# The first two turns of a fused attention and ternary-FFN kernel written out in an order of their own, with two weight quarters loaded to other places and Sign in place of Relu and clip

## The reference, cut to what matters

```python
# x: (8, 1024, 512); 8 heads of 64; segments of 128 tokens, walked in order with a memory per head
q, k, v = xs @ Wq, xs @ Wk, xs @ Wv
att_mem = (elu(q)+1) @ mem / ((elu(q)+1) @ z)          # mem, z: of the segments before
mem += (elu(k)+1).T @ v ;  z += (elu(k)+1).sum()
att = sigmoid(betas) * att_mem + (1 - sigmoid(betas)) * (softmax(q @ k.T / 8) @ v)
x = layernorm(x + att.reshape(...) @ Wo)
Wq1, Wq2 = clip(round(W / (mean(|W|) + 1e-5)), -1, 1)   # W1: 2048x512, W2: 512x2048
out = layernorm(x + relu(x @ Wq1.T + b1) @ Wq2.T + b2)
```

## Time and profile before

| | us |
|---|---|
| median of 3 runs (1894.05 to 1895.91) | 1894.54 |
| the profiled execution's own time | 1894.47 |
| its span, first to last instruction | 1892.5 |
| PE busy in the span | 1848.2 (98%) |
| DVE busy | 1450.5 (77%) |
| ACT busy | 1001.9 (53%) |
| POOL busy | 765.2 (40%) |

### The profile page before, as it was taken

The page is one execution under the profiler, slowest core; times in us unless marked ns, Lnnn a source line. Parts: engine busy times, 40 slices in busy tenths (PEclk is TensorE's granted clock), DMA queues, the critical chain, the costliest instruction groups (busy, mean ns, idle before and its releaser), DMA issues.

```text
span 1892.5 us, 44351 instructions
## 1 busy us (share of the span) xinstructions
PE 1848.2 (98%) x16447; PEld 1306.4 (69%) x16447; DVE 1450.5 (77%) x2935; ACT 1001.9 (53%) x2422; POOL 765.2 (40%) x775
## 2 busy tenths in 40 slices
PE   5789999999999999999999999999999999999998
PEld 3666677776667776667776677776677776677765
DVE  7868777778777778777777777778777778777774
ACT  5765555555555555555555555555555555555541
POOL 1214334444334444334444334444334444344442
PEclk9899999999999999999999999999999999999999
DMA  8422333422333323323322333323333323233110
GB/s 272 125 44 33 62 58 62 68 48 52 63 59 60 68 44 55 64 55 64 68 47 51 64 59 60 68 48 52 60 62 60 68 47 52 59 59 63 36 24 23
DMA packets 556420, 117.47 MB, mean 62 GB/s; under 512 B 529824, under 2 KB 533808, under 8 KB 555696
## 3 DMA queue, kind: packets, MB, share of 16 engines
q1 hardware_dynamic: 556208, 114.64, 30.9%
HBM read 50.54 MB, written 16.80 MB: 36 GB/s over the span
## 4 chain that ended last, share of the span: by engine, by line
PE 93%; DVE 4%; ACT 1%; SPq 1%; issue 1%; DMA 0%; another core or an unknown queue 0%; POOLq 0%; DVEq 0%; POOL 0%; ACTq 0%
PE bank L433 12%; PE bank L434 12%; PE bank L449 11%; PE bank L450 11%; PE bank L282 6%; PE bank L283 6%; PE bank L284 6%; PE bank L370 3%; PE bank L415 3%; PE bank L414 3%; PE bank L413 3%; PE bank L296 3%; PE bank L349 3%; PE bank L298 3%; PE bank L297 3%; PE bank L401 2%
## 5 line engine op out<-in xcount | busy, mean ns | idle before, releaser
L433 PE MATMUL bank<-yt,w1t 128*128 128x256 f16 x2048 | 453.9, 273 | 0.3 <-DVE yt L811 0.2
L434 PE MATMUL bank<-yt,w1t 128*128 128x256 f16 x2048 | 453.9, 273 | 0.0
L1154 ACT ACTIVATE prob<-bank,exp_bias,gscalars 128x128 f32<-128x128 f32 x512 | 227.7, 456 | 360.4 <-DVE exp_bias L728 356.2
L449 PE MATMUL bank<-w2t,arena 128*128 128x512 f16 x1024 | 388.4, 379 | 0.0
L450 PE MATMUL bank<-w2t,arena 128*128 128x512 f16 x1024 | 388.1, 379 | 0.0
L1198 ACT ACTIVATE arena<-bank,b_scaled,wscalars 128x256 f32<-128x256 f32 x512 | 263.0, 570 | 205.3 <-PE bank L434 151.8
L863 DVE CAST arena<-arena 128x512 f16<-128x512 f32 x256 | 154.3, 603 | 92.8 <-ACT arena L1198 92.0
L1323 POOL TENSOR_TENSOR att_mem<-att_mem,gate_in 128x512 f32<-128x512 f32 x60 | 86.6, 1444 | 330.5 <-DVE att_mem L767 320.2
L433 PEld LDWEIGHTS bank<-yt,w1t 128*128 128x128 f16 x2048 | 200.5, 98 | 23.8 <-issue 0.6
L434 PEld LDWEIGHTS bank<-yt,w1t 128*128 128x128 f16 x2048 | 200.3, 98 | 22.7
L1401 POOL TENSOR_TENSOR arena<-arena 128x512 f16<-128x512 f32 x128 | 155.2, 1213 | 86.1 <-DVE arena L863 86.1
(11 more groups left out here) (186 smaller groups left out, 4299.9 us busy)
## 6 DMA issues: line engine op xcount, KB each, us to landing
rows<-in_L_attn_x SPq DMA_DIRECT2D x32, 512.0 KB, 3.8
out_rows<-rows SPq DMA_DIRECT2D x64, 256.0 KB, 2.3
x_blocks<-in_L_attn_x SPq DMA_DIRECT2D x248, 64.0 KB, 3.0
sk<-sk_t SPq DMA_DIRECT2D x480, 32.0 KB, 2.0
att_dot<-att_mem SPq DMA_DIRECT2D x480, 32.0 KB, 2.0
y_blocks<-rows SPq DMA_DIRECT2D x480, 32.0 KB
arena<-in_L_ffn_W SPq DMA_DIRECT2D x6, 1024.0 KB, 5.3
w2t<-in_L_ffn_W SPq DMA_DIRECT2D x2, 1024.0 KB, 13.1
```

Source lines behind the costliest of these rows:

```text
L433: pe.matmul(ps[:, c], w1t[:, k, cols], yt[:, g % 2, :, k], start=k == 0, stop=False)
L434: ins = pe.matmul(ps[:, c], w1t[:, k, cols], yt[:, g % 2, :, KT + k], start=False, stop=k == KT - 1)
L449: pe.matmul(banks[own][:], h_hi[:, f, toks], w2t[:, f, :], start=f == 0, stop=False)
L1154: ins = act.activation(prob[:, t, at], ps[:, c], ACT.Exp, scale=gcol(g, G_EXP), bias=exp_bias[:, t, at:at + 1], accum_out=row_sum[:, t, h: ...
```

## The change

It does four things. It takes turns 0 and 1 out of the loops of PE, DVE and ACT (these now run from g = 2) and writes them out as lists; SP and POOL keep their loop, with some jobs in other places. It handles the largest values of Wq and Wv in one chain, so there are three. It loads the quarters (2, 1) and (2, 3) of W2 into yt and into rows[:, 1:3] instead of arena slots, drops the two extra copies of W2, and sums five quarters on ACT and three on DVE. And it brings the turned blocks out with Sign, whose result is already -1, 0 or 1, so that `clip_w` is gone.

```diff
+        CHAINS = ("k", "qv", "o")
-        SUM_ORDER = [(1, 1), (1, 3), (1, 0), (1, 2), (2, 0), (2, 1)]
+        SUM_ORDER = [(1, 1), (1, 0), (1, 3), (2, 0), (2, 2)]
+        SUM_ORDER_DVE = [(1, 2), (2, 1), (2, 3)]
@@ def ffn_raw(m, i):
+            if (m, i) == (2, 1):
+                return yt[:].rearrange("p g t k n -> p (g t k n)").bitcast(F32)
+            if (m, i) == (2, 3):
+                return rows[:, 1:3].rearrange("p g t d -> p (g t d)")
@@ PE: def ffn_up, def ffn_down: they wait for wput instead of clipped
@@ PE, the list of turns 0 and 1 (after spread_max(0))
+            project_qk(0, "k", 0)
+            turn_max(1); turn_bias(); spread_max(1)
+            project_qk(0, "k", 1); project_qk(0, "q", 0); project_qk(0, "q", 1)
+            project_v(0, 0); project_v(0, 1); scores(0, 0); scores(0, 1)
+            turn_bias_max(); turn_p(0, 0, 0); turn_p(0, 0, 1); sum_all(1); turn_p(0, 1, 0)
+            turn_w 0 to 3; turn_p(0, 1, 1); attend(0, 0)
+            turn_w 4 to 7; turn_max(2); attend(0, 1); spread_max(2)
+            turn_w 8 to 11
+            update_memory(0, 0); update_memory(0, 1); spread_bias_max()
+            project_qk(1, "k", 0)
+            turn_w 12 to 15; turn_att(0, 0); project_qk(1, "k", 1)
+            sum_all(2)
+            project_qk(1, "q", 0)
+            turn_w 16 to 19; project_qk(1, "q", 1); turn_att(0, 1)
+            turn_w 20 to 23; project_out(0, 0); project_out(0, 1)
+            turn_w 24 to 27; scores(1, 0); project_v(1, 0)
+            turn_w 28 to 31; project_v(1, 1); turn_p(1, 0, 0); scores(1, 1)
+            turn_p(1, 0, 1); turn_p(1, 1, 0); turn_y(0, 0); turn_p(1, 1, 1); turn_y(0, 1)
+            attend(1, 0); attend(1, 1); ffn_up(0, 0)
+            for g in range(2, NG + 2):
@@ DVE, the list (after w_split of k)
+            w_max("q"); w_max("v"); w_chain(1); w_scale(1); scalars(0, 0 to 2)
+            w_split("q", 0); w_split("q", 1); qk_split(0, "k", 0); w_split("v", 0); w_split("v", 1)
+            qk_split(0, "k", 1); qk_split(0, "q", 0); gates(); bias_rows_max(); qk_split(0, "q", 1)
+            v_split(0, 0); v_split(0, 1); score_max(0, 0, 0); (0, 0, 1); (0, 1, 0); (0, 1, 1)
+            group_max(1); bias_all_max(); w_sum(1, 2); p_split(0, 0, 0); threshold(1)
+            round_w(0); p_split(0, 0, 1); round_w(1); p_split(0, 1, 0)
+            turn_x(1, 0); turn_x(1, 1); p_split(0, 1, 1); w_max("o")
+            invert_sums(0, 0); (0, 1); scale_sums(0, 0); (0, 1); round_w(2); w_chain(2)
+            all_max(1); x_scale(1, 0 to 3); w_scale(2)
+            att_scale(0, 0)
+            turn_sk(0)
+            att_scale(0, 1); xt_lo(1, 0); xt_lo(1, 1); round_w(3); scalars(1, 0); w_sum(2, 1)
+            scalars(1, 1); (0, 3); (1, 2); (1, 3); w_sum(2, 3); ffn_scale()
+            mem_add(0, 0); mem_add(0, 1); qk_split(1, "k", 0); at_lo(0, 0); qk_split(1, "k", 1)
+            threshold(2); round_w(4); qk_split(1, "q", 0); round_w(5); qk_split(1, "q", 1)
+            at_lo(0, 1); round_w(6); residual(0, 0, 0); round_w(7); residual(0, 1, 0)
+            score_max(1, 0, 0); group_max(2)
...
@@ ACT, the list (after w_split of k)
+            w_sum(1, 1); w_sum(1, 0); w_split("q", 0); w_split("q", 1); qk_split(0, "k", 0)
+            w_split("v", 0); w_split("v", 1); qk_split(0, "k", 1); gates()
+            qk_split(0, "q", 0); qk_split(0, "q", 1); v_split(0, 0); v_split(0, 1); w_sum(1, 3)
+            exponentials(0, 0, 0); (0, 0, 1); p_split(0, 0, 0); exponentials(0, 1, 0)
+            p_split(0, 0, 1); exponentials(0, 1, 1); p_split(0, 1, 0)
+            put_w 0 to 3; p_split(0, 1, 1); put_w 4 to 7; w_sum(2, 0); xt_hi(1, 0); xt_hi(1, 1)
+            put_w 8 to 11; w_split("o", 0); w_split("o", 1); qk_split(1, "k", 0)
+            put_w 12 to 15; at_hi(0, 0); qk_split(1, "k", 1); w_sum(2, 2); qk_split(1, "q", 0)
+            put_w 16 to 19; at_hi(0, 1); qk_split(1, "q", 1); put_w 20 to 27
+            exponentials(1, 0, 0); v_split(1, 0); exponentials(1, 0, 1); put_w 28 to 31
...
@@ ACT: def put_w
-                act.activation(dst, ps, ACT.Relu, bias=unround[:]).then_inc(sem["wput"], 1)
+                act.activation(dst, ps, ACT.Sign, bias=unround[:]).then_inc(sem["wput"], 1)
@@ SP
+                if g == 1:                       # load_x(1)
+                    sp.wait_ge(sem["wturn"], NBLOCKS)
...
             load_ffn_w(1, 1)
+            load_ffn_w(1, 0)
+            load_ffn_w(1, 2)                     # waits for the split of k
             load_w("o")
             load_ffn_w(1, 3)                     # waits for the split of q
+            load_blocks(1)
+            load_ffn_w(2, 1)
+            load_ffn_w(2, 0)                     # waits for the split of v
+            gates_out()
+            load_ffn_w(2, 3)
...
+            gates_back()
             for g in range(NG + 2):
+                if g:
+                    load_blocks(g + 1)
                 bounce_out(g + 1)
                 move_y(g - 1)
                 bounce_back(g + 1)
+                move_sk(g)
+                if g == 0:
+                    load_ffn_w(2, 2)             # waits for wturn 12
                 move_att(g)
                 put_out(g - 2, 0)
+                put_out(g - 2, 1)
+                if g == 1:
                     load_x(1)
                     load_x(2)
                 if g >= 1:
                     load_x(g + 2)
```

More of the change, by code:

```diff
@@ new lines, in _ @@
+            score_max(0, 0, 1)
+            score_max(0, 1, 0)
+            score_max(0, 1, 1)
+            group_max(1)
+            bias_all_max()
+            w_sum(1, 2)
+            p_split(0, 0, 0)
+            threshold(1)
+            round_w(0)
+            p_split(0, 0, 1)
+            round_w(1)
+            p_split(0, 1, 0)
+            turn_x(1, 0)
+            turn_x(1, 1)
+            p_split(0, 1, 1)
+            w_max("o")
+            invert_sums(0, 0)
+            invert_sums(0, 1)
@@ new lines, in _ @@
+            scale_sums(0, 0)
+            scale_sums(0, 1)
+            round_w(2)
+            w_chain(2)
+            all_max(1)
+            x_scale(1, 0)
+            x_scale(1, 1)
+            x_scale(1, 2)
+            x_scale(1, 3)
+            w_scale(2)
+            att_scale(0, 0)
+            turn_sk(0)
+            att_scale(0, 1)
+            xt_lo(1, 0)
+            xt_lo(1, 1)
+            round_w(3)
+            scalars(1, 0)
+            w_sum(2, 1)
+            scalars(1, 1)
+            scalars(0, 3)
@@ new lines, in _ @@
+            scalars(1, 2)
+            scalars(1, 3)
+            w_sum(2, 3)
+            ffn_scale()
+            mem_add(0, 0)
+            mem_add(0, 1)
+            qk_split(1, "k", 0)
+            at_lo(0, 0)
+            qk_split(1, "k", 1)
+            threshold(2)
+            round_w(4)
+            qk_split(1, "q", 0)
+            round_w(5)
+            qk_split(1, "q", 1)
+            at_lo(0, 1)
+            round_w(6)
+            residual(0, 0, 0)
+            round_w(7)
+            residual(0, 1, 0)
@@ new lines, in _ @@
+            score_max(1, 0, 0)
+            group_max(2)
+            normalise(0, 0, 0)
+            normalise(0, 1, 0)
+            score_max(1, 0, 1)
+            turn_x(2, 0)
+            turn_x(2, 1)
+            turn_sk(1)
+            v_split(1, 0)
+            invert_sums(1, 0)
+            p_split(1, 0, 0)
+            v_split(1, 1)
+            score_max(1, 1, 0)
+            score_max(1, 1, 1)
+            invert_sums(1, 1)
+            scale_sums(1, 0)
+            scale_sums(1, 1)
@@ new lines, in _ @@
+            p_split(1, 0, 1)
+            p_split(1, 1, 0)
+            all_max(2)
+            x_scale(2, 0)
+            yt_lo(0, 0)
+            p_split(1, 1, 1)
+            x_scale(2, 1)
+            x_scale(2, 2)
+            x_scale(2, 3)
+            yt_lo(0, 1)
+            att_scale(1, 0)
+            xt_lo(2, 0)
+            att_scale(1, 1)
+            xt_lo(2, 1)
+            h_split(0, 0)
+            mem_add(1, 0)
+            scalars(2, 0)
+            h_split(0, 1)
+            scalars(2, 1)
@@ L981, in _ @@
+            h_split(0, 2)
+            scalars(2, 2)
+            scalars(2, 3)
+            h_split(0, 3)
+            for g in range(2, NG + 2):
                 mem_add(g - 1, 1)
```

426 lines of the change are left out of this document (196 added, 230 removed).

## The result

The changed kernel takes 1907.12 us (median of 5 runs, 1903.85 to 1908.07), the kernel before 1894.87 (5 runs beside it). The ratio is 1.0062, 95% interval 1.0051 to 1.0073: slower by 0.6%. The forecast was 1906.5. The profiled execution is the shortest of the five: 1903.85 us, span 1902.1.

The account below looks back on a forecast made before the run. PE is full from the FFN's first product on, so only that product's start counts; waits between engines ahead of it delay it by 12.1 us. 1894.47 + 12.1 = 1906.6, forecast 1906.5 us, range 1890 to 1914.

Parts of the forecast that it names:

- two waits that the prediction named: PE idle 10 to 13 us near 63 to 76 for sk's DMAs, and about 4 us ahead of `sum_all(2)`'s product.
- Nothing behind the first product moves by itself: From `ffn_up(0, 0)` at 120.35 PE is busy 1764.40 of 1765.65 us, so only that product's start can move.
- `turn_sk(0)` ends at 63: On DVE in turn 0, behind 22.6 us of listed work and a wait, where before it stood at 51.47.
- 16 moves of 10.5 us, blocks in at 75.6: SP's sk DMAs behind `turn_sk(0)`: 10.50 us of issues plus 2.0 to landing, with PE waiting at `update_memory(0, 0)`.
- 1.15 for the update and 0.4 for the bias product: PE's work between sk's landing and `project_qk(1, "k", 0)`, which was to start at 77.3, against 80.36 before.
- The first k half at 1.2 GHz, 4.7 us: Turn 1: after 12 us without work PE's half projection runs slow for 4 us, 4.7 instead of 2.6.
- Blocks 12 to 15, 3.6 us: Moved into turn 1 between the k halves; their banks wait for ACT's `put_w` behind the k split, costing 3.6 us.
- `sum_all(2)`, 4.1 us and the clock behind it, 2.3: Between k and q in turn 1, PE idles 4.1 us for quarter (2, 2)'s sum; a slow next half adds 2.3.
- From the scores of group 1 on as before, 20.5 us: From `scores(1, 0)` to `ffn_up(0, 0)`: the old list with four blocks instead of eight still takes 20.5 us.
- First product at 132.5, 12.1 later: The walk's end: `ffn_up(0, 0)` starts at 132.5 instead of 120.35, the whole predicted loss.
- Sign, the clips, the loads and Wo on POOL cost or bring nothing: Sign priced as Relu's 0.58, seven `clip_w` of 0.60 beside other work, later x loads and POOL's split covered: no effect.
- Rival 1: At `update_memory(0, 0)`: sk's blocks don't hold PE and the clock stays up; -4.6 us, 1890; chance 0.20.

Follow-up runs that it names:

- sk_early: Changed kernel with `turn_sk(0)` on DVE ahead of group 0's second q split and its 16 moves ahead of `bounce_back(1)` on SP; 1896.1 us, ratio 1.0009.
- sk_late_before: Kernel before with `turn_sk(0)` put behind `att_scale(0, 0)` and four loads issued ahead of its 16 moves; 1906.8 us, ratio 1.0065.
- blocks_ahead: Changed kernel with blocks 12 to 15 turned ahead of the memory update and put ahead of group 1's first k split; 1905.4 us, ratio 1.0057.
- sum_early: Changed kernel with quarter (2, 2)'s sum on ACT and `threshold(2)` on DVE ahead of group 1's second k split; 1901.7 us, ratio 1.0036.
- tail_late: Changed kernel with sk's moves and quarter (2, 2)'s sum and threshold earlier, and blocks 28 to 31 back at their old place; 1891.4 us, ratio 0.9978.
- second profile: Changed kernel executed once more, unaltered, for another profile; that profile is of 1907.06 us, the median of its 2 executions 1908.4 us.
- both_early: Changed kernel with the edits of sk_early and sum_early together; 1892.3 us, ratio 0.9988.
- best: tail_late with `round_w(4)` ahead of DVE's second k split of group 1, and blocks 12 and 13 ahead of the first k half; 1889.3 us, ratio 0.9972.

## Why the prediction was right

The forecast was 1906.5 and the median is 1907.1. The two waits that the prediction named are there, and each was removed by an experiment that gave about its price. Point by point, with the profiled execution:
- *Nothing behind the first product moves by itself.* True to about 3 us. PE is full there in each profile but for single waits of up to 1.9 us. The prediction had read the 1.25 idle us of one execution as a constant, but this differed between two executions of the changed kernel by 2.5 us.
- *`turn_sk(0)` ends at 63.* It ended at 62.1. DVE waited 1.90 us for the hi part, which ACT makes behind `put_w` 0 to 3 (foreseen as 0.2 to 1.3), and less for ACT before 40.
- *16 moves of 10.5 us, blocks in at 75.6.* 10.44 us; PE went on at 74.09, 1.5 us sooner. Of this, 0.9 is the earlier `turn_sk(0)`. The other 0.6 is an error: the prediction added the 2.0 us to landing to the end of the last issue, and they count from its start. Shown by sk_early and sk_late_before to be the largest part of the loss: 11.0 us of 12.2.
- *1.15 for the update and 0.4 for the bias product.* The two took 2.45 us, 0.9 more, because the update ran at half clock (2.00 us against 1.15).
- *The first k half at 1.2 GHz, 4.7 us.* The clock was at 0.50 when it began at 76.5, and the half took 3.1. From 77.6 on its products start every 0.11 us, as at 2.4 GHz; by then PE had worked without a pause since 74.09, first on the update. The prediction had let the slow time begin only with the half.
- *Blocks 12 to 15, 3.6 us.* Between the two k halves 4.2 us passed, where 0.4 had: 3.7 more, 1.61 of it idle for ACT. So the term was right in size. What moving the blocks away is worth is not shown to be as much: blocks_ahead gave 2.3 us at `sum_all(2)` and 1.4 at the first product, and its median, 1.7 lower, is not clear of the noise.
- *`sum_all(2)`, 4.1 us and the clock behind it, 2.3.* 3.98 us, and the q half took 4.3 in place of 2.6, so 1.7. sum_early brought back 5.4 in the median and 3.4 at the first product. Shown.
- *From the scores of group 1 on as before, 20.5 us.* 20.8, but by two errors that cancel. The prediction called the list the old one, with four blocks less that would not matter. With the old list and four blocks less, as tail_late has it, 18.6 us pass, not 20.5. And the list is not the old one: the four puts of blocks 28 to 31 now stand on ACT ahead of the splits of the probabilities, PE idled 2.49 and 2.38 us in place of 1.15 and 1.04, and then ran at half clock, which costs the 2.2 us that tail_late takes back. That this term fits is luck.
- *First product at 132.5, 12.1 later.* It was at 129.7, 9.3 later, and in the second profile at 130.4. The walk was 2 to 3 us too late: 1.6 us in the k half, 0.7 in the q half and 1.5 in the blocks of sk, less the 0.9 of the update. The second profile, at the median's time, has 2.5 us more behind the first product than the first one, which the walk had not. So the near hit of 1906.5 on 1907.1 owes something to these two cancelling, which is luck. The mechanism doesn't: each of its two waits was taken away by itself, and one put in by itself.
- *Sign, the clips, the loads and Wo on POOL cost or bring nothing.* Shown for Sign and the clips. Of the eight clips five lay ahead of the first product before, the last at 91.00, and three at 148; the prediction's seven is a miscount. POOL, the x rows and the other loads were not tried by themselves; no wait in the profile after names them.
- *Rival 1*, the faster one, had its condition met in sk_early and came out at 1896.1 in place of 1890, the first product 5.0 us later than its sum (115.8). It had the clock up everywhere, but the clock stood at 0.50 from 64 to 68 there too, after idle stretches of only 1.53 and 1.87 us. PE came to the update 2.0 us later than the rival had it and took 0.9 longer for it and the bias product, and the q half behind the 3.98 us of idleness took 4.3 in place of 2.6.

What the written-out order is worth without its two late jobs: both_early is 2 to 3 us under the kernel before, best 5 to 6. Part of the 16 us by which DVE and ACT were ready earlier was only work put off to turn 1: blocks 12 to 19, 3.5 us of PE by the prediction's price, and the second threshold. How the rest divides between the joined chain, the dropped clips and sums and the new order was not tried.

## What to carry to other kernels

When an order is written by hand over engines that each run in order, follow every job that has a DMA behind it to the first engine that needs the data, and place it by the time of that landing and not by the engine's free slots: 1.2 us of work here had 12 us of issues and landing behind it. A step that all partitions meet in, like a threshold, wants its last input early enough that PE finds it; else PE idles and then runs at half clock. And an early job is worth what it brings at the place where the full engine starts, so read a change there first, and then in the time.

## What was not expected of the hardware

- The clock was back sooner than the prediction took: in the changed kernel it stood at 0.50 until 76 and was at 0.80 from 76 to 80, with PE working since 74.09. It also fell in the softmax of group 1 (0.50 from 124 to 128) after idle stretches of 2.49 and 2.38 us, where the kernel before, with stretches of 1.15 and 1.04 us, kept 1.00. In tail_late about the same idle time in seven shorter stretches left it at 1.00.
- Two executions of the same program differ by 2.5 us behind the first product; the longer one has three waits (3.1 us together) that the shorter lacks.
